# Ordering the last mixture-of-experts tiles by sample, joining twelve samples beside the last eight tiles, and moving the join's last operation to VectorE

## The reference

```python
probs = softmax(xf @ gate_w + gate_b)
gates, expert_idx = top_k(probs, 2)
h = relu(einsum('nc,ech->neh', xf, w1) + b1)
expert_out = einsum('neh,ehc->nec', h, w2) + b2
out = sum over the two chosen experts of gate * expert_out
x = layernorm(x + out)          # (x - m) / sqrt(v + 1e-5), no scale, no shift
```

## Time and profile before

| | us |
|---|---|
| median of 3 runs | 996.99 (995.23 to 997.38) |
| the profiled execution | 998.28 |
| its span | 995.2 |
| PE busy | 868.6 (87%) |
| DVE / ACT / POOL busy | 615.4 / 497.9 / 297.1 |

### The profile page before, as it was taken

One profiled execution on the slowest core, in us unless ns is written; L12 is line 12 of the kernel. 1 busy time (PEld: TensorE's weight loads), 2 busy tenths in 40 slices (PEclk: granted clock), 3 DMA queues, 4 the chain that ended last, 5 costly groups with the idle time before them and its releaser, 6 DMA issues.

```text
span 995.2 us, 19709 instructions
## 1 busy us (share of the span) xinstructions
PE 868.6 (87%) x7316; PEld 688.7 (69%) x7316; DVE 615.4 (62%) x1840; ACT 497.9 (50%) x1159; POOL 297.1 (30%) x478
## 2 busy tenths in 40 slices
PE   3669899999999899999999999999999999299950
PEld 2446668667777666777678777877877888289940
DVE  4998776676765768866848685778854434200016
ACT  2335446553656454553465545565555555045535
POOL 4423322222343123431213333232421214212236
PEclk9679999999999989999999999999999999689985
DMA  8996000000010000000000030231121226699836
GB/s 323 400 323 210 2 1 12 12 7 17 17 33 28 18 7 17 22 22 17 6 2 22 23 118 23 91 118 54 55 84 54 92 91 212 225 318 351 321 129 235
DMA packets 35950, 102.33 MB, mean 103 GB/s; under 512 B 4984, under 2 KB 20352, under 8 KB 35296
## 3 DMA queue, kind: packets, MB, share of 16 engines
q1 hardware_dynamic: 32448, 91.74, 27.0%
q0 software_dynamic: 3408, 9.34, 2.5%
HBM read 87.53 MB, written 33.35 MB: 121 GB/s over the span
## 4 chain that ended last, share of the span: by engine, by line
PE 63%; DVE 19%; ACT 7%; issue 6%; DMA 3%; POOL 1%; SPq 0%; ACTq 0%; DVEq 0%; POOLq 0%
PE ps L705 44%; PE ps L710 7%; PE ps L717 5%; PE ps L781 3%; DVE PT L1104 2%; DVE stat L1045 2%; ACT PT L1438 2%; ACT slot_rows L1438 1%; PE ps L848 1%; DMA xs_d<-X,idx 1%; PE ps L1006 1%; DVE sm L1061 1%; DVE PT L1069 1%; DMA KB<-xs_d 1%; DVE stat L1046 1%
## 5 line engine op out<-in xcount | busy, mean ns | idle before, releaser
L1626 POOL TENSOR_TENSOR stat<-stat,mhalf 128x1 f32<-128x1 f32 x112 | 67.1, 599 | 291.2 <-DVE stat L1047 291.1
L705 PE MATMUL ps<-wall,slot_rows 128*128 128x256 f32 (+1 forms) x448 | 132.3, 424 | 11.3 <-ACT KB L1465 8.9
L705 PEld LDWEIGHTS ps<-wall,slot_rows 128*128 128x128 f32 x448 | 79.1, 193 | 36.0 <-issue 22.8
L710 PE MATMUL ps<-cst,PT 128*128 128x128 f32 x512 | 73.4, 280 | 14.9 <-DVE PT L1104 4.2
L717 PE MATMUL ps<-KB 32*128 32x128 f32 (+1 forms) x2048 | 76.9, 287 | 7.2 <-DVE PT L1104 2.4
L1104 DVE TENSOR_REDUCE PT<-ps 128x8 f32<-128x1024 f32 x64 | 75.3, 1219 | 12.5 <-PE ps L717 12.4
L705 PE MATMUL ps<-wgu,slot_rows 128*128 128x352 f32 x256 | 82.1, 473 | 0.8 <-ACT slot_rows L1400 0.6
L717 PEld LDWEIGHTS ps<-KB 32*128 32x128 f32 (+1 forms) x2048 | 64.9, 190 | 25.7 <-issue 20.6
L705 PEld LDWEIGHTS ps<-slot_rows,wall 128*128 128x128 f32 x640 | 75.8, 193 | 8.5 <-issue 4.1
L705 PE MATMUL ps<-slot_rows,wall 128*128 128x128 f32 x640 | 79.6, 279 | 1.8 <-DVE KB L1165 0.9
L710 PEld LDWEIGHTS ps<-cst,PT 128*128 128x128 f32 x512 | 58.7, 143 | 30.6 <-issue 16.2
(11 more groups left out here) (237 smaller groups left out, 1817.5 us busy)
## 6 DMA issues: line engine op xcount, KB each, us to landing
EW<-moe_w SPq DMA_DIRECT2D x23, 514.0 KB, 4.3
EW<-moe_w SPq DMA_DIRECT2D x23, 512.0 KB, 5.0
PT<-moe_w SPq DMA_DIRECT2D x12, 514.0 KB, 5.9
PT<-moe_w SPq DMA_DIRECT2D x12, 512.0 KB, 6.9
wall<-wts SPq DMA_DIRECT2D x1, 4104.0 KB, 20.4
work<-xs_d SPq DMA_DIRECT2D x25, 129.0 KB, 3.3
KB<-ys_d SPq DMA_DIRECT2D x8, 384.0 KB, 5.9
slot_rows<-ys_d SPq DMA_DIRECT2D x8, 384.0 KB, 9.3
```

Source lines behind the costliest of these rows:

```text
L705: last = k.e.matmul(o, a, b, start=(i == 0), stop=(i == len(pairs) - 1))
L710: last = k.e.transpose(ps[:, u.at, c * P:(c + 1) * P], src[:, c * P:(c + 1) * P], ident)
L1626: return k.e.tensor_tensor(v[:, 7:8], v[:, 8:9], mhalf[:, :], ALU.pow)
```

## The change

- `SEEN` is 12 (the samples of all steps but the last), `SHOWN` is 2 * 12 + 7 = 31: the number of tiles that surely holds all pairs of the first twelve samples. At the table after sample 12, `dve_counts` also notes in `seen` each expert's number of tiles rounded up. The last table then has sixteen entries instead of eight: first what is left of each expert's `seen` tiles, then the rest of each expert. So tiles 0 to 30 hold all pairs of samples 0 to 11.
- The fetches of samples 0 to 11 wait for the stores of tiles 0 to 30 only, and join, add and finish of these samples come before those of the last four. The fetches of samples 12 to 15 stand after join 11 in `join_turns` and wait for all stores.
- "finish" is one DVE instruction (subtract the mean, multiply) instead of two of ACT; DVE's negation of the mean (line 1367) goes.
- `join_rows` puts samples 0 to 9 into `slot_rows`, and 10 to 15 into `KB_all` from its end down.
- `plan_join` has new costs for the planner. PE's order is unchanged, ACT's only loses the join.

```diff
+SEEN = STEPS[-2]
+SHOWN = 2 * SEEN + E - 1
...
 def join_turns():
-    yield from (("fetch", n) for n in range(B))
-    yield "add", 0
-    for n in range(B):
-        if n < B - 1:
-            yield "add", n + 1
-        yield "join", n
-        if n:
-            yield "finish", n - 1
-    yield "finish", B - 1
+    for lo, hi in ((0, SEEN), (SEEN, B)):
+        if not lo:
+            yield from (("fetch", n) for n in range(lo, hi))
+        yield "add", lo
+        for n in range(lo, hi):
+            if n < hi - 1:
+                yield "add", n + 1
+            yield "join", n
+            if n == SEEN - 1:
+                yield from (("fetch", m) for m in range(SEEN, B))
+            if n > lo:
+                yield "finish", n - 1
+        yield "finish", hi - 1
+
+def tiles_of(n):
+    return SHOWN if n < SEEN else NT
...
+        def dve_counts(k, out, half):
+            e = k.e
+            k.after(k.step(e.tensor_tensor(out, base[:, :], k_("region")[:, 0:E], ALU.subtract)))
+            k.after(k.step(e.tensor_scalar(out, out, 1.0 / P, half, ALU.mult, ALU.add)))
+            k.after(k.step(e.tensor_scalar(out, out, ROUND, None, ALU.add)))
+            k.after(k.step(e.tensor_scalar(out, out, ROUND, None, ALU.subtract)))
...
         def dve_table(k, t):
+            parts = 1 if full else 2
+            wide = parts * E
...
+            else:
+                k.step(e.tensor_tensor(c[:, E:wide], c[:, E:wide], seen, ALU.subtract))
+                k.after(k.step(e.tensor_tensor(c[:, 0:E], seen, had, ALU.subtract)))
...
+            if not full:
+                k.after(k.step(e.tensor_scalar(gone, owner, float(E), -float(E), ALU.is_ge, ALU.mult)))
+                k.after(k.step(e.tensor_tensor(owner, owner, gone, ALU.add)))
...
+            if STEPS[t] == SEEN:
+                dve_counts(k, seen, half)
...
         def dve_join(k):
...
-                    e.tensor_scalar(v[:, 6:7], v[:, 6:7], -1.0, None, ALU.mult).then_inc(var6, 1)
+                elif what == "finish":
+                    k.wait_ge(root6, n + 1)
+                    e.tensor_scalar(x6, x6, v[:, 6:7], v[:, 7:8], ALU.subtract, ALU.mult).then_inc(out_ready, 1)
...
         def sp_join(k):
...
-                    for x in range(NT):
+                    for x in range(tiles_of(n)):
```

More of the change, by code:

```diff
@@ L376, in plan_join @@
             yield piece(work=[("S", 0.5, None), ("Q", 1.1, None), ("L", 2.4, (n, "fetched"))], alone=True,
[L377 removed]
+                        needs=[(n, "saved"), ("table", len(STEPS) - 1), *(("stored", x) for x in range(tiles_of(n)))])
         elif what == "join":
[L379 to L380 removed]
+            yield piece(work=[("D", 1.2, None), ("P", 0.57, (n, "last root"))], needs=[(n, "halved")], alone=True)
         elif what == "add":
@@ L1299, in dve_router @@
                     yield
+        def dve_counts(k, out, half):
[4 more added lines that the diff above has]
+            k.after(k.step(e.tensor_scalar(out, out, ROUND, None, ALU.subtract)))
         def dve_table(k, t):
             e, nt, full = k.e, TILES[t], t < len(STEPS) - 1
-            c, end, begin, step, had, row0 = (cnt[:, i, 0:E] for i in range(6))
-            region, top = k_("region"), float(E * REGION // P)
-            hit, tiles = below[0:1, 0:nt, :], k_("tiles")[0:1, 0:nt]
+            parts = 1 if full else 2
+            wide = parts * E
+            c, end, begin, step, gone0, row0 = (cnt[:, i, 0:wide] for i in range(6))
+            had, seen = cnt[:, 4, 0:E], cnt[:, 4, E:2 * E]
+            region, top = k_("region")[:, 0:wide], float(E * REGION // P)
+            late = v3(w("oT")[:, 0:nt * wide], wide)
+            hit, tiles = (below[0:1, 0:nt, :] if full else late[0:1, :, :]), k_("tiles")[0:1, 0:nt]
             owner, gone, rows_ = (tcol[0:1, i, 0:nt] for i in range(3))
@@ L1311, in dve_table @@
             k.wait_ge(emptied[u.at], u.out)
[L1312 to L1320, removed]
+            dve_counts(k, c[:, wide - E:wide], -half if full else half)
+            if full:
+                if t:
+                    k.after(k.step(e.tensor_tensor(c, c, had, ALU.subtract)))
+            else:
+                k.step(e.tensor_tensor(c[:, E:wide], c[:, E:wide], seen, ALU.subtract))
+                k.after(k.step(e.tensor_tensor(c[:, 0:E], seen, had, ALU.subtract)))
+            k.after(k.step(e.tensor_tensor_scan(end, ones[:, 0:wide], c, 0.0, ALU.mult, ALU.add)))
+            k.step(e.tensor_tensor(hit, bc(end[0:1, :].unsqueeze(1), nt, wide), bc(tiles.unsqueeze(2), nt, wide), ALU.is_le))
+            k.step(e.tensor_scalar(cnt[:, 5, wide:wide + 1], end[:, wide - 1:wide], -1.0, top, ALU.mult, ALU.add))
             k.after(k.step(e.tensor_tensor(begin, end, c, ALU.subtract)))
@@ L1582, in act_bias @@
                 yield
[L1584 to L1590, removed]
-                    k.wait_ge(centred, n + 1)
-                    k.wait_ge(root6, n + 1)
-                    k.e.activation(x6, x6, ACT.Identity, scale=v[:, 7:8], bias=0.0).then_inc(out_ready, 1)
-                yield
         def act_tiles(k):
```

40 lines of the change are left out of this document (21 added, 19 removed).

## The result

| | before | after |
|---|---|---|
| median (13 runs each) | 996.53 us (993.48 to 999.24) | 989.97 us (985.09 to 992.59) |
| the profiled execution | 998.28 | 988.44 |
| its span | 995.2 | 986.5 |

The ratio of the times is 0.9934 (95% interval 0.9918 to 0.9951): 6.6 us faster (4.9 to 8.2), where 12.0 were forecast. The direction is right. The median lies inside the range (982.5 to 990.0) by 0.03 us only, and that is luck: the runs themselves spread over 7.5 us, and 0.9934 of the 996.99 us that the forecast started from would be 990.4. A second set of runs of the changed kernel (experiment 10) gave 0.9933. One execution of experiment 4 (1679 us) and one of experiment 10 (3043 us) were slow beyond all others and are in no ratio or median here.

What follows compares the result with a forecast made beforehand. Bound by PE on tiles, then a 24.4 us join of sixteen samples. Join -13.4, last table +1.2, table after sample 12 +0.2: -12.0 us, from 996.99 to 985.0, range 982.5 to 990; this forecast's chance 0.76.

Steps and rivals of the forecast that it cites:

- three signs of being wrong: POOL finds its fetches missing for long, tile 38's store starts beyond 968, or PE stands still before that store.
- Rivals 3 (slower): SP's queue: tile 38's second-half weights wait far longer behind twelve fetches; about 1001 us at 150 GB/s; chance 0.02.
- 4 (nothing hidden): Early join: fetches wait for late stores after all, or nothing is hidden; 1000 us; chance 0.02.
- add 0, from tile 38's start: First early add on POOL, relative to PE's first product of tile 38: forecast at -10.6 us.
- POOL, add 0 to store of tile 38: POOL's queue: 12 adds, 10 roots, five stores, 19.5 us plus 0.8 lost; store 3.0 late.
- that store to the end of the last finish: Last four samples: store at 962.7, add 12 at 968.4, DVE-bound samples, last finish ending at 976.4.
- finish; one sample on DVE: In the join's last samples, the finish takes 0.406 us like line 1056, and one sample costs DVE 1.6.
- gain of the join: End of the join moves from 989.77 to 976.4, so 13.4 us are gained.
- table: Last table before `tab_ready`: longer operations cost +1.2 us, all of it counting since PE is idle; bounds 0.8 and 2.
- lands about 942.4: First early fetch: bytes move from 941.0 after a backlog worked off at 403 GB/s, landing about 942.4.
- Rival 1: POOL and DVE hold each other up, each finish costing the other 0.41 us; 991.5 us; chance 0.10.
- free by then: SP's queue: the ten stores to `out` are no longer waiting, as finish 9 comes before store 38.

Runs made afterwards that it cites:

- experiment 10: The changed kernel, not edited, timed again; ratio to the kernel before 0.9933 (0.9908 to 0.9957).
- experiment 4: The changed kernel with the second half of tile 38's weights issued ahead of the twelve early fetches on SP; ratio to before 0.9947.
- experiment 3: The changed kernel with the finish as two ACT instructions again, and DVE's negation; ratio to before 0.9938.
- experiment 1: The kernel before with only the finish changed to one DVE instruction; ratio to before 1.0017 (1.0002 to 1.0033).
- experiment 2: The changed kernel without the early join: new table and DVE finish, old join order, all fetches waiting for all 39 tiles; ratio to before 1.0046.
- experiment 5: The changed kernel with POOL's order alone rewritten, the stores of tiles 33 to 38 standing where each tile is ready; ratio to before 0.9935.
- experiment 9: Experiment 5 with the last four fetches behind the output of sample 6 on SP instead of sample 9; ratio to before 0.9923.
- experiment 7: Experiment 6 with one row over all sixteen samples, last fetches behind join 8, last two tiles' places ahead of the joins; ratio to before 0.9895.
- experiment 6: The changed kernel with the edits of experiments 4 and 5 together; ratio to before 0.9938 (0.9923 to 0.9953).

## Why the prediction was right, and where it was off

The path was right: twelve samples run beside the last tiles, the price is paid on POOL, the store of tile 38 is late through POOL's queue and not through its data, and the rest of the join takes what was forecast. The forecast time was right only in part, since the gain was a little over half of the 12.0. Two sizes were off, and of the three signs of being wrong that the prediction names, two showed: POOL missed its fetches for 4.50 us ahead of add 0, and PE stood still for 1.22 us before the second half of tile 38, where "one under 1 us" was allowed. The store of tile 38 stayed below 968. Rivals 3 (slower) and 4 (nothing hidden) are out by the ratio and by add 0 at 945.00, while PE multiplied until 959.9.

| step | forecast | measured |
|---|---|---|
| add 0, from tile 38's start | -10.6 | -8.05, -8.43 |
| POOL, add 0 to store of tile 38 | 20.3 | 22.05, 22.05 |
| that store to the end of the last finish | 13.7 | 13.77, 14.35 |
| finish; one sample on DVE | 0.41; 1.6 | 0.40; 1.52 |
| gain of the join | 13.4 | 9.0, 8.8 |
| table | 1.2 | 1.36 on DVE |

1. **The first fetch** was 2.2 to 2.6 us later than "lands about 942.4". It was issued at 938.98, 0.6 after the 938.4 forecast, and took 6.0 to the first add instead of 4.0. I had worked off the queue at the 403 GB/s that fetches reach, but while weights and fetches go together the rate was 349 (the stretch 940 to 945 above), and the trace of before showed 347 for such a stretch. By the prediction's own sum that is only some 0.5 us (1.03 MB and one fetch). The larger part is that it let the first fetch land alone and ahead of the others. By the DMA records 2.10 MB moved between its issue and its landing: 0.60 MB of weights, 0.25 of stores, and 1.22 of fetches, which is 3.1 fetches. SP issued the fetches some 0.6 us apart, faster than they moved. A fetch raises its semaphore in sixteen parts, and those of fetch 0 came spread over 941.77 to 944.93; the first fetch of the join before had them within 964.84 to 965.27. So ten parts of sixteen were there by 942.33, near the forecast, and the add waits for the last. The trace of before had a row for it too, the last weights, issued at 938.40 behind the same backlog; the last number is the time to landing:

```profile
KB<-moe_w SPq DMA_DIRECT2D x1, 512.0 KB, 5.3
```

2. **POOL's queue** took 1.75 us more than its sum. POOL was busy for 20.16 us instead of 19.5: five stores of 1.04 to 1.17 us instead of 0.96 are 0.8, ten roots at 0.63 instead of 0.60 are 0.3 and the adds 0.2, less some 0.6 by which the records overlap. And it stood for 1.9 us instead of the 0.8 charged: 0.15 to 0.18 of issue ahead of each of six stores are 1.0, waits of roots for DVE 0.7. The wait charged at the start, add 0 done before store 33 has its data, did not come, as add 0 was late.

   Rival 1 is there at its small end. The Trainium skill (GPSIMD Engine Reference, Key points), cited there for contention between GpSimd and VectorE, is borne out in direction: POOL's add takes up to 0.93 us and DVE's finish up to 1.26, each beside work of the other, while the medians stay at 0.72 and 0.40. The prediction held against this rival that the adds before are beside just such inputs without harm, and that was misread. Before, fifteen of the sixteen adds run beside no `tensor_tensor` of DVE but beside BATCH_NORM_STATS2, which has one input, and the small instructions behind it; the one add that meets a `tensor_tensor` (at 966.31) took 0.79 for 0.72. The first pair below is from the kernel before, the second from the changed kernel:

```profile
975.01 0.72 POOL L1766 TENSOR_TENSOR KB<-KB 128x256 f32<-128x256 f32 x1
975.03 0.43 DVE L1364 BATCH_NORM_STATS2 mv<-KB 128x6 f32<-128x256 f32 x1
...
960.87 0.71 POOL L1789 TENSOR_TENSOR slot_rows<-slot_rows 128x256 f32<-128x256 f32 x1
960.93 1.25 DVE L1402 TENSOR_SCALAR slot_rows<-slot_rows,mv 128x256 f32<-128x256 f32 x1 [0.36 <-POOL mv L1649]
```

   In all twelve profiles every finish or `tensor_tensor` of DVE that overlaps an add of POOL by more than 0.15 us is stretched or stretches the add, and no BATCH_NORM_STATS2 is (0.43 us under a whole add). By experiment 3, where it is the `tensor_tensor` that meets the adds (four of 0.70 to 0.72), it isn't the finish in particular.

3. **The finish** came out at the duration of line 1056, and the rule on float32 tensor_scalar (the Trainium skill, VectorE: DVE Perf Modes, Mode 2×_2P) again isn't what the trace shows: 0.40 us against 0.42 for the tensor_tensor of the same shape. The sample on DVE is 1.52 and not 1.6, since instructions behind one another start 0.08 before the record of the one ahead ends (experiment 1).
4. **The table.** From `idx` to the last column of `tab` it is 3.99 us before (853.51 to 857.50) and 5.35 after (854.11 to 859.46), 1.36 more; the four operations on 352 elements take 0.51 each for 0.33 before, 0.18 more where 0.19 was forecast. In the medians the table is within 0.6 to 5.2 us (experiments 1 and 2). All twelve profiles together are sharper: from the start of `idx` to PE's first transpose of the last step it is 19.32 and 19.54 us in the two kernels with the old table and 20.24 to 20.73 in the ten with the new one, 1.0 more on average, so nothing further hides behind it. In the first profile of the changed kernel it doesn't show at tile 38, which starts at 953.05 for 953.00: the first transpose came 1.37 us later than before, and from there to tile 38 it took 1.32 less, all of it in the first two sets of sixteen products (2.99 and 1.95 us for 3.78 and 2.32), as the clock rose early. Such shifts are also why the two profiled executions differ by 9.8 us and the medians by 6.6; the clock is 1.3 of these 3.2, the rest isn't told apart. The second profile of the changed kernel is 5.5 below that of before, and the mean of the two is 7.7.

In sum, 12.0 forecast less 2.6 and 1.75 for the two sizes, and less 0.3 for a way from the last finish to the end of 5.7 us instead of 5.4, is 7.4. It lies inside the interval of the measured 6.6 (4.9 to 8.2); what is behind the last 0.8 isn't told apart.

The prediction's last section asks for the first add "near 943.5 + 1.4 = 944 us". That is 944.9, and 942.4 stands in its sum; that the add came at 945.00 confirms the first number by chance only. The prediction also missed that SP's queue is a second wait, 2.0 us shorter than the first. I wrote of the ten outputs on SP that they are "free by then", and it was so only because the store was late: with the store earlier, and the finishes later for it, they are what holds the last fetches (experiments 5 and 9).

## What to carry to other kernels

When a stage is moved beside another, its in-order queue carries both, and its price is the sum of all pieces on that engine, with the issue times that idle gaps used to hide; put the pieces that others wait for where they are due, and look for the wait that comes next, since mending one can lengthen the other and show no gain. Take the landing of a transfer behind a backlog from a transfer that stood at that place, not from bytes over a rate: here the last of its sixteen parts came 3.2 us behind the first, while others that were issued behind it moved. "They ran side by side without harm" has to be read from which instructions overlap, not from both engines being busy. Measure stages from a fixed point nearby in the same profile, as one profiled execution can differ from the next by more than the change is worth.

## What was not expected of the hardware

- The point at which TensorE's granted clock rises from 0.50 to 1.00 after some 20 us of idleness differs between executions of one kernel: the first sixteen products took 2.99 us in one and 3.79 in another, so the tiles behind them shift by 1 us.
- POOL's indirect store of 128 rows takes 0.96 us when POOL had been waiting, and 1.04 to 1.17 with 0.15 to 0.20 of issue ahead of it when it stands between vector operations. In a row of adds and roots one store costs some 1.2 us (experiment 7).
- DVE's `tensor_tensor` of 128x256 took 0.42 us as a rule and 0.70 to 0.96 in a few cases beside POOL's work, its finish 0.40 and up to 1.41 (experiments 5, 6 and 9), and POOL's add 0.77 to 0.94 for 0.72. The pairs are POOL's add with one of these two; BATCH_NORM_STATS2 beside an add stayed at 0.43. No run moves such a pair apart by itself, so its price in the time isn't known.
- A fetch issued behind a backlog landed in sixteen parts spread over 3.2 us (941.77 to 944.93), where the first fetch of the join before, on quiet queues, had them within 0.4 us.
